# A 16-sequence cross-attention block on one core: the order of the first slots, of eight weight refills and of one pair of FFN gates

## The chip, the cores and the metric

One core of a Trainium2 chip runs the whole block. The metric is the device time of one launch in microseconds (us), the median of the runs. The kernel drives five engines by hand-written streams: TensorE (PE), VectorE (DVE), ScalarE (ACT), GpSimd (POOL) and SyncE (SP, which only issues transfers).

## The reference

For each of B = 16 sequences of S = 256 rows and D = 256 columns, with context `cond` of 256 rows and 192 columns (16 heads of 64, so 8 pairs of heads; everything is float32):

```
h = layernorm(x) * g1 + b1
x = softmax((h wq)(h wk)^T / 8) (h wv) wo + bo + x        # self attention
h = layernorm(x) * g2 + b2
x = softmax((h cq)(cond ck)^T / 8) (cond cv) co + cbo + x # cross attention
h = layernorm(x) * g3 + b3
a, gate = split(h w1 + fb1)                                # 1024 + 1024
out = (a * gelu(gate)) w2 + fb2 + x
```

Each float32 product is made on TensorE from rounded (high) and residual (low) parts in the type fp32r: three matmuls high x high, high x low, low x high. So every operand is written twice: once rounded (usually by ScalarE), once as the difference (VectorE or GpSimd).

## The kernel before

**Slots.** Attention is a software pipeline of `ATT` = 256 slots, one for each pair of heads of each sequence: 128 for self attention, 128 for cross attention. Slot c of an engine's stream holds that engine's part for several units at once. A unit k is the query and key product of one pair. In slot c, TensorE makes the scores of unit c (`pe_scores`), the query and key product of unit c + 3 (`pe_project`; later c + 7), a part of the values (`pe_value_turn`), the output product of unit c - 4 (`pe_outputs`), the transposes of the probabilities of c - 1 (`pe_transposes`), and probabilities times values of c - 2 (`pe_heads`). VectorE takes the maxima of the scores (`NM`), ScalarE the exponentials (`PT`, L791), TensorE transposes them into `PTB`, ScalarE rounds them into `PH` (L819), VectorE makes the low part `PL` (`dve_p_low`, L897). ScalarE and VectorE also copy and split each product into `QKS` (`act_copy_qk`, L722; `dve_split_qk`, L903). GpSimd normalizes the outputs (`ON` times `RB`, L1189) and splits them into `OT` (L1192, L1194), which `pe_outputs` reads.

**Two ways to the scores.** From unit 3 on (`DIRECT`), SP copies the parts of `QKS` with four transfers per unit into the ring `RX` (`copy_ring`, L683 and L685) in a layout with both parts stacked, and the scores read the ring. The units 0 to 2 are read straight from `QKS` (L454). `unit(k)` names the place in `QKS`; here units 2 and 3 have places of their own (0 and 1), so their products can be copied and split before the scores of units 0 and 1 are done.

**The first slots** run from c = -3. The weights arrive in twelve pieces, which are rounded by ScalarE (`act_weights`, L1526) and split by VectorE (`dve_weights`) and GpSimd (`pool_low`, L1559). The rows of sequence 1 go through the first layernorm beside them: statistics, `dve_normalize` (L858) into `XN`, a store to DRAM (`store_rows`, SP), a load that turns them (`act_load_rows`, four transfers on ScalarE's queue, L691), a transpose of 32 x 32 blocks (`dve_turn_rows`, L876), gain and bias (ScalarE), and the split into `HT` (`pool_split_h`, GpSimd). Unit 8 is the first to need them. Here the normalization lies behind the weight split of slot 0 for its first tile and in slot 1 for its second; the store is issued in slot 1, the load in slot 2, and the block transpose is in slot 3.

**The end of attention.** Weights for the next phase were split and stored to DRAM earlier. `fill_weights` (SP) refills `WQ` a quarter at a time, four chunks of 256 KB, one per slot (L1697). The quarters 2 and 3 for the FFN are refilled from slot `LAST` = 248 to 256, behind the ring copies in SP's order. The FFN processes chunks of two sequences in eight units each; `pe_gates(c)` makes both halves of unit c (4.2 us with its second product in the steady state), ScalarE's Gelu and VectorE turn them into `FH`, high and low (L1472, L1474), and `pe_second(s)` multiplies by `w2` (L1352). Units 0 to 3 are made early by `pe_raw` (L1295) in the last attention slots. Behind the last slot TensorE's order is written out by hand:

```
pe_gates(e, EARLY)
pe_heads(e, Slot(ATT + 1, ATT))
pe_outputs(e, ATT - 3)
pe_second(e, 0)
pe_second(e, 1)
pe_outputs(e, ATT - 2)
pe_gates(e, EARLY + 1)
```

What sets the order everywhere is the order in which each stream is written, with semaphores between the streams. SP, ACT and the others each run their stream in order, so an instruction that waits holds all behind it on its engine.

Of the kernel before, what the change touches and what calls it, by code (L numbers as in the profile page):

```python
# [19 lines left out]
PAIRS = H // 2  # L20
# [54 lines left out]
def first_alone(k):  # L75

    return 0 <= k < OLD
# [7 lines left out]
def joint(j):  # L85

    return OLD <= j < LAST
# [20 lines left out]
def unit(k):  # L108

    if last_alone(k):  # L110
        return (7, 1, 2, 0, 3, 4, 5, 6)[k - LAST]
    if alone(k):
        return k - 2 if DIRECT - 1 <= k <= DIRECT else (3, 7)[k % 2]
    n, p = place(k)
    u = n // 2 * PAIRS + p
    return 3 + u % 5 if n % 2 else u % 3
# [97 lines left out]
def block_kernel(nc, x, ctxt, ln1_g, ln1_b, ln2_g, ln2_b, ln3_g, ln3_b, sa_wq, sa_wk, sa_wv, sa_wo,  # L214
                 sa_bo, ca_wq, ca_wk, ca_wv, ca_wo, ca_bo, ff_w1, ff_b1, ff_w2, ff_b2, out):
    ctx = ExitStack()
    with ctx:
# [373 lines left out]

        def pe_slot(e, sl):
            c = sl.c
            late = c == 1 or joint(c + LEAD) and first_alone(c + AHEAD)
            if joint(c + LEAD):
                pe_project_both(e, c + LEAD)
            if c == 2:
                pe_value_turn(e, c)
            if first_alone(c + AHEAD) and not late:
                pe_project(e, c + AHEAD)  # L600
            if last_alone(c + LEAD):
                pe_project(e, c + LEAD)
            if ATT <= c + LEAD < ATT + RAWS:
                pe_raw(e, c + LEAD - ATT)

            if 0 <= c < ATT and not 2 <= c <= 3:
                pe_value_turn(e, c)
            if c == -2:
                pe_values(e, 0)

            pe_outputs(e, c - 4)
            pe_transposes(e, sl)

            if late:
                pe_project(e, c + AHEAD)

            pe_heads(e, sl)
# [94 lines left out]
        def act_copy_qk(e, k):  # L712

            e.wait_ge(a.pe_qk, nth_alone(k) + 1)
            if k >= LAST:
                held = max(m for m in range(DIRECT, k) if unit(m) == unit(k))
                e.wait_ge(d_dup[held % 2], 16 * COPIES * copied(held))
            elif k > DIRECT + 2:
                e.wait_ge(d_dup[k % 2], 16 * COPIES * copied(k - 2))
            elif k > DIRECT:  # L720
                e.wait_ge(a.pe_s, 2 * (k - DIRECT))
            e.activation(QKS[:, unit(k), 0:2, :], qk_bank(k)[:, :].rearrange("p (u s) -> p u s", u=2), ACT.Copy) \  # L722
                .then_inc(a.act_hi, 1)

# [30 lines left out]
        def act_slot(e, sl):  # L755
# [15 lines left out]
            if due(c, 1, 2):  # L771
                act_load_rows(e, due(c, 1), 0, 1)
            for k in range(KD):
                if due(c, 3 + k, 2):
                    act_gain_bias(e, due(c, 3 + k), k)
                if c == DIRECT + 1:
                    act_gain_bias(e, 1, k)
            for k in range(3):
                if due(c, k - 5, B):
                    act_load_ctx(e, due(c, k - 5, B), *((0,), (3,), (6, 7))[k])  # L780

            if sl.has(c):
                sl.wait(e, a.pe_t, c - 1)
# [12 lines left out]

            if c == 0:
                act_copy_qk(e, 2)
            if first_alone(c + AHEAD) and not late and c != -1:
                act_copy_qk(e, c + AHEAD)  # L800
            if joint(c + LEAD) and not late:
                act_copy_both(e, c + LEAD)
# [22 lines left out]
            if late:  # L825
                act_copy_qk(e, c + AHEAD)

            if due(c, 1, 2):
                act_load_rows(e, due(c, 1), 2, 3)
            if c == DIRECT - 1:  # L830
                act_load_rows(e, 1, 0, 1, 2, 3)
            for k in range(2):
                if due(c, k - 5, B):
                    act_load_ctx(e, due(c, k - 5, B), *((1, 2), (4, 5))[k])
# [94 lines left out]
        def dve_rows(e, sl):  # L929

            c = sl.c
            if due(c, 2, 2):
                dve_turn_rows(e, due(c, 2))
            if c == DIRECT:
                dve_turn_rows(e, 1)
            if due(c, -2, B):
                dve_turn_ctx(e, due(c, -2, B))
            n = normalized_in(c)
            if n:
                e.wait_ge(a.dve_th, n - 1)  # L940
# [32 lines left out]
            if ATT - 7 <= c < ATT - 3:  # L973
                dve_normalize(e, zero_ffn, fs, 1, ROWS, (c - ATT + 7,))

        def dve_reciprocal(e, sl, s):

            e.wait_ge(a.act_exp, 2 * s + 2)
            if s > 1:
                e.wait_ge(d_ds[(s - 2) % 4], 16 * ((s - 2) // 4 + 1))  # L980
            if s == 1:
                e.wait_ge(a.dve_rt, 1)
            e.reciprocal(RDEN[:, 0:4], DEN[:, s % 2, :]).then_inc(a.dve_rc, 1)
            e.wait_ge(a.dve_rc, s + 1)
            e.transpose(RDT[:, s % 2, :], RDEN[:, :]).then_inc(a.dve_rt, 1)

        def dve_slot(e, sl):
            c = sl.c
            late = joint(c + LEAD) and first_alone(c + AHEAD)
# [6 lines left out]
                                    AX.X, ALU.max, negate=True).then_inc(a.dve_nm, 1)  # L996

            if c == 0:
                dve_weights(e, 5)
                e.wait_ge(a.pe_h, 2)  # L1000
                dve_normalize(e, sl, a, 1, (near(1),), (0,))
                dve_split_qk(e, 2)
            if c == 1:
                dve_reciprocal(e, sl, 0)

            if c > 2 and sl.has(c - 2) and c < ATT - 1:
                dve_p_low(e, c - 2, 1)
# [9 lines left out]
            if 0 <= c + 1 < FIRST_V:  # L1017
# [1 line left out]
                sl.wait(e, a.pe_v, v + 1)  # L1019
                sl.wait(e, a.pl_v, v - 3)  # L1020
                e.tensor_copy(VF[:, v // 2 % 2, v % 2, :], VB[:, 0:S]).then_inc(a.dve_vf, 1)
            if c == 1:
                dve_normalize(e, sl, a, 1, (near(1),), (1,))
            if c == 2:
                dve_weights(e, 9)

            if late:
                dve_split_both(e, c + LEAD)
# [3 lines left out]
            dve_rows(e, sl)  # L1032
            dve_ffn_rows(e, c)

            if sl.has(c) and c > 0:
                dve_reciprocal(e, sl, c)

            if first_alone(c + AHEAD) and not late and c != -1:
                dve_split_qk(e, c + AHEAD)
            if joint(c + LEAD) and not late:  # L1040
                dve_split_both(e, c + LEAD)
# [114 lines left out]
        def pool_slot(e, sl):  # L1156
# [14 lines left out]
                if due(c, k - 1, B):  # L1171
                    pool_split_ctx(e, sl, due(c, k - 1, B), k)
            for k in range(KD):
                if due(c, 3 + k, 2):
                    pool_split_h(e, sl, due(c, 3 + k), k)
                if c == DIRECT + 1:
                    pool_split_h(e, sl, 1, k)
            pool_weights(e, c)
            for t in range(TT):
                if due(c, 5 + t):  # L1180
# [318 lines left out]
        def pe_attention_slot(e, sl):  # L1499
            if sl.c == -1:  # L1500
                pe_scores(e, Slot(0, ATT))
            if sl.c == 3:
                pe_value_turn(e, 3)
            if sl.c > 0:
                pe_scores(e, sl)
            pe_slot(e, sl)
# [22 lines left out]
        def dve_weights(e, *ns):  # L1529

            for n in ns:
# [5 lines left out]
                else:  # L1537
                    e.tensor_tensor(low, raw(n), hi, ALU.subtract).then_inc(s_wlo, 1)

        def act_attention_slot(e, sl):  # L1540
            act_slot(e, sl)
            if -AHEAD <= sl.c < 3:
                act_weights(e, *((4,), (5,), (6, 7), (8,), (9, 10), (11,))[sl.c + AHEAD])
            if sl.c == PAIRS * 2:
                e.wait_ge(d_sm, 16 * 5)
                e.activation(LNG[:, 1, :, :], LNG[:, 1, :, :], ACT.Copy, scale=SCALE).then_inc(s_gain, 1)
# [39 lines left out]
        def _(e):  # L1586
# [117 lines left out]
            def fill_weights(c):  # L1704
# [4 lines left out]
                if pair in HALVES and B + 1 <= seq <= B + 2 * NCH:  # L1709
                    store_split(QTR * NCH + 2 * (seq - B - 1) + HALVES.index(pair))  # L1710
                for phase, first in ((0, SLOTS), (1, ATT)):
                    for quarter in range(QTR):
                        if phase and quarter >= 2:
                            freed = nth_alone(ATT - QUAD + 2 * quarter - 3) + 1
                            at = LAST + 4 * (quarter - 2)
                            turns = ((0, 1, 2, 3), (0, 1, 3, 4))[quarter - 2]
                        else:
                            j = first - 2 * PAIRS + 4 * quarter + 3
                            freed = nth_joint(j) + 1
                            at = j - LEAD + 2  # L1720
                            turns = (0, 1, 2, 3)
                        for chunk in range(4):
                            if c == at + turns[chunk]:
                                if chunk == 0:
                                    await_stored(phase)
                                    e.wait_ge(a.pe_qk, freed)
                                    if quarter > 1:
                                        e.wait_ge(d_wq[quarter % 2], 16 * 4 * (QTR // 2 * phase + quarter // 2))
# [54 lines left out]
            for c in range(-AHEAD, ATT + 2):  # L1783
# [10 lines left out]
                if 0 <= c - 1 + AHEAD < ATT and c - 1 >= -AHEAD:  # L1794
                    k = c - 1 + AHEAD
                    if k >= DIRECT:
                        copy_ring(e, k)
                if c == 1:
                    store_rows(1)
                weights(c)  # L1800
                fill_weights(c)
# [81 lines left out]
        def _(e):  # L1883
# [12 lines left out]
            pe_heads(e, Slot(ATT + 1, ATT))  # L1896
            pe_outputs(e, ATT - 3)
            pe_second(e, 0)
            pe_second(e, 1)
            pe_outputs(e, ATT - 2)  # L1900
            pe_gates(e, EARLY + 1)
            pe_second(e, 2)
            pe_outputs(e, ATT - 1)
            pe_second(e, 3)
# [35 lines left out]
```

## Time and profile before

| | |
|---|---|
| median of 3 runs | 1690.47 us (1689.78 to 1691.63) |
| profiled execution, own time | 1689.77 us |
| its span | 1687.9 us |
| PE / DVE / ACT / POOL busy | 1676.3 / 1396.7 / 1249.1 / 1082.0 us |
| transfers | 288.91 MB, mean 171 GB/s |
| granted TensorE clock | 1.000 |

The span is from the first to the last instruction. A busy PE means that a matmul was in flight; the ends of matmuls are modelled, so that two that follow each other overlap by some 0.1 us, and the distance of starts is the better measure of what a group takes. "Idle before" is the time in which an engine had nothing in flight before an instruction, and the releaser is what ended it. Issues of transfers stand under ACTq and SPq with the time that they held the queue.

### The profile page before, as it was taken

What the parts mean: (1) busy time and instruction counts of PE and PEld (TensorE: products, weight loads), DVE (VectorE), ACT (ScalarE), POOL (GpSimd) and SP (SyncE); (2) the same over time, 40 slices, a digit from 0 to 9 for tenths busy, and PEclk for the clock granted to TensorE, in tenths of its full rate; (3) what the DMA queues carried; (4) which work ended last, traced back from release to release, by engine and by line L of the source; (5) the groups of instructions that cost most, each with busy time, mean ns of one, the idle gap of its engine ahead of it and who ended that gap; (6) DMA issues with size and microseconds to landing.
All of it is one profiled execution on the core that took longest, in us unless ns stands there. A gap on an engine that the chain in (4) does not pass through costs nothing.

```text
span 1687.9 us, 39061 instructions
## 1 busy us (share of the span) xinstructions
PE 1676.3 (99%) x11712; PEld 1560.7 (92%) x11712; DVE 1396.7 (83%) x2964; ACT 1249.1 (74%) x3378; POOL 1082.0 (64%) x1804
## 2 busy tenths in 40 slices
PE   8999999999999999999999999999999999999999
PEld 8999999999999999999999999999999998888888
DVE  7888788888888888888888888888888987656665
ACT  7788788888888888888888888888888886232221
POOL 7776577777766667687777777777777564231111
PEclk9999999999999999999999999999999999999999
DMA  7776677777776667887787878787776776112110
GB/s 209 187 181 161 171 197 198 205 202 212 198 181 158 158 166 201 233 221 181 192 211 188 210 198 209 195 207 187 191 188 173 196 209 169 51 50 76 62 39 26
DMA packets 301137, 288.91 MB, mean 171 GB/s; under 512 B 103424, under 2 KB 252032, under 8 KB 300928
## 3 DMA queue, kind: packets, MB, share of 16 engines
q1 hardware_dynamic: 246848, 272.76, 61.9%
q10 hardware_dynamic: 54080, 13.65, 3.6%
q8 instruction: 96, 1.57, 0.4%
q14 instruction: 113, 0.93, 0.2%
HBM read 82.98 MB, written 37.49 MB: 71 GB/s over the span
## 4 chain that ended last, share of the span: by engine, by line
PE 96%; DVE 1%; DMA 1%; SPq 0%; issue 0%; ACT 0%; ACTq 0%; DVEq 0%
PE QKB L564 17%; PE PVB L648 14%; PE PTB L577 13%; PE WOP L630 11%; PE VB L499 9%; PE S L466 7%; PE S L467 7%; PE S L1330 5%; PE PTB L1330 5%; PE QKB L546 3%; PE QKB L1352 3%; PE VB L1352 3%; PE QKB L1295 0%; DMA XR<-in_x_dram 0%; DMA HF<-rows 0%
## 5 line engine op out<-in xcount | busy, mean ns | idle before, releaser
L791 ACT ACTIVATE PT<-S,NM 128x256 f32<-128x256 f32 x1024 | 471.9, 473 | 139.2 <-DVE NM L995 138.5
L897 DVE TENSOR_TENSOR PL<-PTB,PH 128x512 fp32r<-128x512 f32 x512 | 350.8, 686 | 123.8 <-ACT PH L819 122.3
L1189 POOL TENSOR_TENSOR ON<-ON,RB 128x256 f32<-128x256 f32 x256 | 188.5, 736 | 272.2 <-DVE ON L1014 247.8
L995 DVE TENSOR_REDUCE NM<-S 128x2 f32<-128x512 f32 x512 | 327.4, 681 | 1.2 <-PE S L467 1.1
L819 ACT ACTIVATE PH<-PTB 128x1024 fp32r<-128x1024 f32 x256 | 264.0, 1031 | 72.0 <-PE PTB L577 71.1
L577 PE MATMUL PTB<-IDN,PT 128*128 128x128 f32 x2048 | 265.5, 272 | 0.6 <-DVE PL L897 0.5
L466 PE MATMUL S<-RX 128*128 128x256 f32 x1012 | 254.0, 283 | 2.1 <-DMA RX<-QKS 2.1
L467 PE MATMUL S<-RX 128*128 128x256 f32 x1012 | 253.7, 283 | 0.0
L564 PE MATMUL QKB<-HT,WQ 128*128 128x512 f32 x936 | 242.0, 394 | 0.2
L630 PEld LDWEIGHTS WOP<-WO,OT 128*128 128x128 f32 x1536 | 217.5, 190 | 19.7
L577 PEld LDWEIGHTS PTB<-IDN,PT 128*128 128x128 f32 x2048 | 229.6, 140 | 1.3 <-DVE PL L897 0.8
L630 PE MATMUL WOP<-WO,OT 128*128 128x256 f32 x1536 | 224.0, 282 | 0.0
L1014 DVE TENSOR_TENSOR ON<-PVB,ON 64x256 f32<-64x256 f32 x512 | 213.5, 417 | 3.9 <-ACT ON L766 0.3
L766 ACT ACTIVATE ON<-PVB 64x256 f32<-64x256 f32 x512 | 194.5, 380 | 17.9 <-issue 3.1
L791 ACT ACTIVATION_READ_ACCUMULATOR PT<-S,NM 128x1 f32 x1024 | 207.5, 203 | 0.0
L1194 POOL TENSOR_TENSOR OT<-ON,OT 128x256 fp32r<-128x256 f32 x256 | 190.3, 744 | 20.5
L1168 POOL TENSOR_TENSOR VR<-VF,VR 128x256 fp32r<-128x256 f32 x256 | 189.8, 741 | 20.5
L466 PEld LDWEIGHTS S<-RX 128*128 128x128 f32 x1012 | 193.4, 191 | 2.5 <-DMA RX<-QKS 2.5
L467 PEld LDWEIGHTS S<-RX 128*128 128x128 f32 x1012 | 194.2, 192 | 0.0
L564 PEld LDWEIGHTS QKB<-HT,WQ 128*128 128x128 f32 x936 | 165.9, 189 | 27.8 <-DVE QKS L911 0.6
L648 PE MATMUL PVB<-PH,VR 128*128 128x256 f32 x1024 | 183.5, 300 | 0.4 <-issue 0.4
L648 PE MATMUL PVB<-PL,VR 128*128 128x256 f32 x1024 | 163.4, 282 | 0.0
(162 smaller groups left out, 2921.8 us busy)
## 6 DMA issues: line engine op xcount, KB each, us to landing
RX<-QKS SPq DMA_DIRECT2D x506, 192.0 KB, 2.9
RX<-QKS SPq DMA_DIRECT2D x506, 128.0 KB, 2.8
RB<-denominators SPq DMA_DIRECT2D x512, 64.0 KB, 2.7
out_dram<-XR SPq DMA_DIRECT2D x32, 256.0 KB, 3.4
weights_qk<-SPL SPq DMA_DIRECT2D x32, 256.0 KB, 3.4
WQ<-weights_qk SPq DMA_DIRECT2D x32, 256.0 KB, 3.3
rows<-XN SPq DMA_DIRECT2D x23, 256.0 KB, 2.7
rows<-HF SPq DMA_DIRECT2D x22, 256.0 KB, 2.7
```

Source lines behind the costliest of these rows:

```text
L466: e.matmul(o, q, RX[:, c % 2, i, K1, :], start=True, stop=False)
L467: last = e.matmul(o, q, RX[:, c % 2, i, K2, :], start=False, stop=True)
L564: last = e.matmul(QKB[:, :], w_pair(w, wp, p), act, start=i == 0, stop=i == len(passes) - 1)
L577: last = e.transpose(PTB[:, i, kt * S + qt * P:kt * S + (qt + 1) * P], PT[:, s % 2, q0:q0 + P], IDN[:, :])
L630: last = e.matmul(WOP[:, t * D:(t + 1) * D], OT[:, op, t * P:(t + 1) * P], WO[:, p, wp, :], start=begins(s) and t == 0 and j == 0, stop=en ...
L648: last = e.matmul(PVB[:, i * S:(i + 1) * S], VR[:, s // 2 % 2, kt, s % 2, i * P:(i + 1) * P], part[:, first:first + S], start=i == 0 and j ...
L766: last = e.activation(ON[OWN[i], s % 2, :], PVB[OTHER[i], i * S:(i + 1) * S], ACT.Copy)
L791: last = e.activation(PT[:, c % 2, j * S:(j + 1) * S], S1[:, i, qt * S:(qt + 1) * S], ACT.Exp, bias=NM[:, j:j + 1], accum_out=DEN[:, c % 2 ...
L819: e.activation(PH[:, s % 2, :], PTB[:, :, :].rearrange("p i n -> p (i n)"), ACT.Copy) \
L897: e.tensor_tensor(PL[:, cols], PTB[:, i, :], PH[:, s % 2, cols].bitcast(F32), ALU.subtract).then_inc(a.dve_pl, 1)
L995: e.tensor_reduce(NM[:, i * TT:(i + 1) * TT], S1[:, i, :].rearrange("p (t s) -> p t s", t=TT), AX.X, ALU.max, negate=True).then_inc(a.dve_ ...
L1014: last = e.tensor_tensor(on, PVB[OWN[i], i * S:(i + 1) * S], on, ALU.add)
```

## The change

- `unit`: all of the first units alternate between the places 3 and 7 of `QKS`; a copy of unit k > 1 now waits for the scores of unit k - 2.
- TensorE: in slot 2 the product of unit 5 goes behind the transposes, as that of unit 4 does in slot 1; the values of slot 2 and 3 stand in their general place.
- ScalarE: the copies of units 3 and 4 stand ahead of the exponentials of slots 1 and 2. The load of the rows of sequence 1 is at the end of slot 1; gain and bias in slots 3 and 4.
- VectorE: in slot 0 both tiles of sequence 1 are normalized right behind the maxima; the low parts of units 3 and 4 stand behind the maxima of slots 1 and 2; the reciprocal of slot 0 is in slot 0; the block transpose is in slot 2.
- SP: the store of the rows of sequence 1 is the first instruction of its slots. GpSimd: `pool_split_h` in slots 3 and 4.
- The last eight `WQ` transfers are issued by ScalarE at the end of its slots 248 to 255 (`act_load_last`).
- `pe_second(e, 1)` stands behind `pe_outputs(e, ATT - 2)` and `pe_gates(e, EARLY + 1)`.

```diff
@@ unit
-        return k - 2 if DIRECT - 1 <= k <= DIRECT else (3, 7)[k % 2]
+        return (3, 7)[k % 2]
@@ pe_slot
-            late = c == 1 or joint(c + LEAD) and first_alone(c + AHEAD)
+            late = 0 < c < DIRECT or joint(c + LEAD) and first_alone(c + AHEAD)
-            if c == 2:
-                pe_value_turn(e, c)
...
-            if 0 <= c < ATT and not 2 <= c <= 3:
+            if 0 <= c < ATT:
                 pe_value_turn(e, c)
@@ act_copy_qk
-            elif k > DIRECT + 2:
+            elif k > DIRECT + 1:
                 e.wait_ge(d_dup[k % 2], 16 * COPIES * copied(k - 2))
-            elif k > DIRECT:
-                e.wait_ge(a.pe_s, 2 * (k - DIRECT))
+            elif k > 1:
+                e.wait_ge(a.pe_s, 2 * (k - 1))
@@ act_slot
+            if 0 < c < DIRECT:
+                act_copy_qk(e, c + 2)
...
-            if first_alone(c + AHEAD) and not late and c != -1:
+            elif first_alone(c + AHEAD) and not late and not -1 <= c < DIRECT - 1:
                 act_copy_qk(e, c + AHEAD)
...
-            if due(c, 1, 2):
-                act_load_rows(e, due(c, 1), 2, 3)
-            if c == DIRECT - 1:
-                act_load_rows(e, 1, 0, 1, 2, 3)
+            if due(c, 1):
+                act_load_rows(e, due(c, 1), *(range(2, 4) if due(c, 1, 2) else range(4)))
@@ dve_rows
-            if due(c, 2, 2):
+            if due(c, 2):
                 dve_turn_rows(e, due(c, 2))
-            if c == DIRECT:
-                dve_turn_rows(e, 1)
@@ dve_slot
             if c == 0:
+                e.wait_ge(a.pe_h, 2)
+                dve_normalize(e, sl, a, 1, (near(1),))
                 dve_weights(e, 5)
-                e.wait_ge(a.pe_h, 2)
-                dve_normalize(e, sl, a, 1, (near(1),), (0,))
-                dve_split_qk(e, 2)
-            if c == 1:
-                dve_reciprocal(e, sl, 0)
+            if 0 < c < DIRECT:
+                dve_split_qk(e, c + 2)
+            if c == 2:
+                dve_weights(e, 9)
...
-            if c == 1:
-                dve_normalize(e, sl, a, 1, (near(1),), (1,))
-            if c == 2:
-                dve_weights(e, 9)
...
+            if c == 0:
+                dve_split_qk(e, 2)
+            elif first_alone(c + AHEAD) and not late and not -1 <= c < DIRECT - 1:
                 dve_split_qk(e, c + AHEAD)
@@ pool_slot
-                if due(c, 3 + k, 2):
+                if due(c, 3 + k):
                     pool_split_h(e, sl, due(c, 3 + k), k)
-                if c == DIRECT + 1:
-                    pool_split_h(e, sl, 1, k)
@@ scalar stream
+        def act_load_last(e, c):
+
+            quarter, chunk = divmod(c - LAST, 4)
+            if 0 <= quarter < 2:
+                if chunk == 0:
+                    for done in d_ws:
+                        e.wait_ge(done, 16 * QTR * NCH)
+                    e.wait_ge(a.pe_qk, nth_alone(ATT - QUAD + 2 * quarter + 1) + 1)
+                    e.wait_ge(d_wq[quarter], 16 * 4 * (QTR // 2 + 1))
+                e.dma_start(WQ[:, 2 + quarter, chunk, :, :].bitcast(F32), WSQ[1, :, 2 + quarter, chunk, :, :]) \
+                    .then_inc(d_wq[quarter], 16)
+
         def act_attention_slot(e, sl):
             act_slot(e, sl)
+            act_load_last(e, sl.c)
@@ sync stream
-                if c == 1:
+                if c == -AHEAD:
                     store_rows(1)
@@ fill_weights
-                    for quarter in range(QTR):
-                        if phase and quarter >= 2:
...
+                    for quarter in range(QTR - 2 * phase):
@@ tensor stream
             pe_second(e, 0)
-            pe_second(e, 1)
             pe_outputs(e, ATT - 2)
             pe_gates(e, EARLY + 1)
+            pe_second(e, 1)
             pe_second(e, 2)
```

## Rows read from the trace of the kernel before

**Rows 1.** The page: busy time of each engine.

```profile
PE 1676.3 (99%) x11712; PEld 1560.7 (92%) x11712; DVE 1396.7 (83%) x2964; ACT 1249.1 (74%) x3378; POOL 1082.0 (64%) x1804
```

**Rows 2.** TensorE's waits over the span: releaser, us in total, times, longest.

```profile
PE S L466 <- DMA RX<-QKS: 2.1, 2, 1.1
PE QKB L1352 <- DVE QKS L1474: 2.0, 1, 2.0
```

**Rows 3.** TensorE's timeline, first slots: start, us, line, out<-in, [idle before].

```profile
19.78 1.68 PE L546 MATMUL QKB<-HT,WQ 128*128 128x256 f32 x12
...
23.21 1.60 PE L546 MATMUL QKB<-HT,WQ 128*128 128x256 f32 x12
...
27.19 0.29 PE L466 MATMUL S<-RX 128*128 128x256 f32 x1
...
34.00 0.39 PE L466 MATMUL S<-RX 128*128 128x256 f32 x1 [0.97 <-DMA RX<-QKS]
...
35.81 1.69 PE L546 MATMUL QKB<-HT,WQ 128*128 128x256 f32 x12 [0.60 <-DVE QKS L903]
...
40.61 0.28 PE L466 MATMUL S<-RX 128*128 128x256 f32 x1
```

**Rows 4.** VectorE's timeline, first slots.

```profile
15.81 1.37 DVE L858 TENSOR_SCALAR XN<-XR,MV,RSTD 128x256 f32<-128x256 f32 x1
...
18.04 0.68 DVE L903 TENSOR_TENSOR QKS<-QKB,QKS 128x512 fp32r<-128x512 f32 x1
18.64 1.27 DVE L995 TENSOR_REDUCE NM<-S 128x2 f32<-128x512 f32 x2
19.84 0.16 DVE L983 RECIPROCAL RDEN<-DEN 128x4 f32<-128x4 f32 x1
...
20.47 0.40 DVE L858 TENSOR_SCALAR XN<-XR,MV,RSTD 128x256 f32<-128x256 f32 x1
...
34.16 0.71 DVE L876 STREAM_TRANSPOSE XN<-HF 128x512 f32<-128x512 f32 x1 [1.96 <-DMA HF<-rows]
```

**Rows 5.** ScalarE's timeline with its queue (ACTq), end of slot 2.

```profile
26.96 0.34 ACTq L691 DMA_DIRECT2D HF<-rows  x1
...
27.34 2.04 ACTq L691 DMA_DIRECT2D HF<-rows  x3
29.43 0.63 ACT L1526 ACTIVATE WV<-XR 128x512 fp32r<-128x512 f32 x1 [1.05 <-issue]
```

**Rows 6.** Stretches: busy us of each engine, granted clock, DMA share, GB/s.

```profile
16.00:20.00 4.00, 3.28 (x33) 2.90 (x32) 4.00 (x7) 2.53 (x8) 3.84 (x6) 1.00 0.10 32
...
28.00:32.00 4.00, 3.22 (x24) 2.59 (x23) 3.73 (x8) 2.89 (x9) 3.08 (x6) 1.00 0.98 247
```

**Rows 7.** SP's queue, first slots: the last copy of unit 4.

```profile
28.65 0.62 SPq L685 DMA_DIRECT2D RX<-QKS  x1
```

**Rows 8.** GpSimd's timeline, first slots.

```profile
30.14 1.27 POOL L1559 TENSOR_TENSOR WV<-XR,WV 128x512 fp32r<-128x512 f32 x1 [0.76 <-ACT WV L1526]
...
33.88 0.73 POOL L1189 TENSOR_TENSOR ON<-ON,RB 128x256 f32<-128x256 f32 x1
```

**Rows 9.** TensorE's timeline, end of attention.

```profile
1407.56 0.39 PE L466 MATMUL S<-RX 128*128 128x256 f32 x1 [1.10 <-DMA RX<-QKS]
...
1430.25 0.98 PE L1352 MATMUL QKB<-WV,QKS 128*128 128x256 f32 x6 [2.01 <-DVE QKS L1474]
```

**Rows 10.** SP's queue, end of attention: the last copy of unit 254, a refill.

```profile
1403.85 0.62 SPq L685 DMA_DIRECT2D RX<-QKS  x1
1404.64 0.46 SPq L1697 DMA_DIRECT2D WQ<-weights_qk  x1
```

**Rows 11.** ScalarE's timeline with its queue, end of attention.

```profile
1390.75 0.35 ACTq L1364 DMA_DIRECT2D rows<-XN  x1
1390.79 0.77 ACT L766 ACTIVATE ON<-PVB 64x256 f32<-64x256 f32 x2
```

**Rows 12.** GpSimd and VectorE behind the last slot.

```profile
1427.31 0.74 POOL L1194 TENSOR_TENSOR OT<-ON,OT 128x256 fp32r<-128x256 f32 x1
...
1429.51 0.69 DVE L1474 TENSOR_TENSOR QKS<-PT,QKS 128x512 fp32r<-128x512 f32 x1
```

More of the change, by code:

```diff
@@ L773, in act_slot @@
             for k in range(KD):
-                if due(c, 3 + k, 2):
+                if due(c, 3 + k):
                     act_gain_bias(e, due(c, 3 + k), k)
-                if c == DIRECT + 1:
-                    act_gain_bias(e, 1, k)
             for k in range(3):
@@ L974, in dve_ffn_rows @@
                 dve_normalize(e, zero_ffn, fs, 1, ROWS, (c - ATT + 7,))
[L976 to L985, printed above, removed]
         def dve_slot(e, sl):
@@ L1033, in dve_slot @@
             dve_ffn_rows(e, c)
-            if sl.has(c) and c > 0:
-                dve_reciprocal(e, sl, c)
-            if first_alone(c + AHEAD) and not late and c != -1:
+            if sl.has(c):
+                sl.wait(e, a.act_exp, 2 * c + 2)
+                if c > 1:
+                    e.wait_ge(d_ds[(c - 2) % 4], 16 * ((c - 2) // 4 + 1))
+                e.reciprocal(RDEN[:, 0:4], DEN[:, c % 2, :]).then_inc(a.dve_rc, 1)
+                sl.wait(e, a.dve_rc, c + 1)
+                e.transpose(RDT[:, c % 2, :], RDEN[:, :]).then_inc(a.dve_rt, 1)
+            if c == 0:
+                dve_split_qk(e, 2)
+            elif first_alone(c + AHEAD) and not late and not -1 <= c < DIRECT - 1:
                 dve_split_qk(e, c + AHEAD)
@@ L1173, in pool_slot @@
             for k in range(KD):
-                if due(c, 3 + k, 2):
+                if due(c, 3 + k):
                     pool_split_h(e, sl, due(c, 3 + k), k)
-                if c == DIRECT + 1:
-                    pool_split_h(e, sl, 1, k)
             pool_weights(e, c)
@@ L1501, in pe_attention_slot @@
                 pe_scores(e, Slot(0, ATT))
-            if sl.c == 3:
-                pe_value_turn(e, 3)
             if sl.c > 0:
@@ L1711, in fill_weights @@
                 for phase, first in ((0, SLOTS), (1, ATT)):
-                    for quarter in range(QTR):
-                        if phase and quarter >= 2:
[L1714 to L1721, printed above, removed]
+                    for quarter in range(QTR - 2 * phase):
+                        j = first - 2 * PAIRS + 4 * quarter + 3
+                        freed = nth_joint(j) + 1
                         for chunk in range(4):
-                            if c == at + turns[chunk]:
+                            if c == j - LEAD + 2 + chunk:
                                 if chunk == 0:
@@ L1727, in fill_weights @@
                                     if quarter > 1:
-                                        e.wait_ge(d_wq[quarter % 2], 16 * 4 * (QTR // 2 * phase + quarter // 2))
+                                        e.wait_ge(d_wq[quarter % 2], 16 * 4)
                                 load_quarter(phase, quarter, chunk)
```

## Prediction

> **What bounds the kernel now.** I read the page first, then TensorE's list of waits, then the timelines of every engine in the first 45 us and from 1370 to 1440 us, and TensorE's row for the middle. The page has PE busy 99% of the span [rows 1], and the granted clock is 1.00 in every stretch asked for [rows 6]: nothing can be gained but PE's own stalls, and only edits that make or remove a stall count. The waits name them: two on the copied units `RX`, one of 2.0 us before a second FFN product [rows 2], and smaller ones of up to 0.6 us. The timelines put all of these either before 41 us or between 1407 and 1431 us. Steady slots are gapless; the slot that starts at 40.61 us is the first of them [rows 3]. So the change, which touches the slots -3 to 4 and the end of attention, is judged at two marks: when the scores of slot 5 start (40.61 us before), and when `pe_gates(EARLY + 1)` and what follows it run. All arithmetic is against the profiled execution: its span is 1687.9 us and its own time 1689.77; the median of the runs shown is 1690.47, 0.7 above it.
>
> **The first slots.** Nothing is touched until slot 0's maxima. Every figure below is a start or an end in us, chained from the rows.
>
> *VectorE, slot 0.* Now both normalizations of sequence 1 come right behind the maxima, from about 15.0. One took 1.37 us there while GpSimd ran, the other 0.40 us [rows 4]. How long the two take in a row is not shown: 0.8 us at best, 2.75 at worst. I take 1.37 + 0.40, because the first lies in the same stretch of GpSimd's weight splits as before. Against before, this slot gets the second tile (0.40) and the reciprocal with its transpose (19.84 to 20.17, 0.33), and loses the split of unit 3 (18.04 to 18.64, 0.60) [rows 4]: the maxima of slot 1 start at 18.64 + 0.40 + 0.33 - 0.60 = 18.77 instead of 18.64, and I leave the exponentials behind them where they were (19.4 to 21.3). The Trainium skill's page "SBUF — State Buffer", section "Who interferes with whom", says that a vector operation in a two-port mode and a GpSimd operation block each other for the whole instruction. The 1.37 us row agrees; by the rule alone the second tile could be held as well, which is the upper bound above.
>
> *Low part of unit 3 behind the maxima.* It is no longer made ahead of slot 1's maxima but behind them: these take 1.20 (18.64 to 19.84 [rows 4]), so it runs from 19.95 to 20.6. The product of unit 4 waits for it: 20.6 instead of 19.78 [rows 3], a loss of 0.8. The scores of slot 2 follow one product (1.44) later, at 22.05.
>
> *ScalarE at the end of slot 1.* The four transfers that fetch the rows of sequence 1 now issue here, behind the rounding of the probabilities. Before, they held ScalarE's queue from 26.96 to 29.38, 2.4 us, and ScalarE resumed at 29.43 [rows 5]. Now they go from 21.0 (the exponentials' last instruction) to 23.4. They wait for the store of these rows, which SP can issue at 16.8 in a stretch in which the transfer engines are 10% busy [rows 6]; so no wait there. SP is held in its first slot until then, and has nothing else queued. Behind the issues ScalarE does two weight roundings (one takes 0.63 [rows 5], two overlapped 1.15) until 24.55, then, new, the copy of unit 4 ahead of the exponentials of slot 2: 24.6 to 25.2. Its low part ends at 25.9, and the product of unit 5, which PE now has behind the transposes, starts there instead of at 23.21. PE has the values and the transposes in between (until 24.7), so it stalls 1.2. Product 1.44 and heads 1.03 give the scores of slot 3 at 28.4 (27.19 before): 1.2 late, the sum of what the edits cost until here.
>
> *What comes back.* (a) Before, VectorE sat 1.96 us, until 34.16, for the fetched rows [rows 4]; they landed 4.7 us behind their last issue, with the transfer engines 98% busy [rows 6]. Now the last issue ends at 23.4, so at the same 4.7 us they are there at 28.1, and VectorE passes at about the time when the copy of unit 5 lets it split anyway (28.1 to 28.75). (b) The last `RX` copy of unit 4 was issued at 28.65 and landed at 34.0 [rows 3, 7]. Now SP issues the four from 25.9 to 28.4, as it has one store less in front. With the same 4.7 us they land at 33.1. (c) PE: scores until 29.35, product of unit 6 until 30.8, values 31.5, transposes 32.3 (low part of slot 1's probabilities done 31.55, so the 0.5 us stall goes), heads 33.35, scores of slot 4 at 33.35 instead of 34.00. (d) The product of unit 7 waited 0.6 until 35.81, because unit 6 was split behind the late rows [rows 3, 4]. Now the exponentials of slot 3 end at 32.95, copy and split follow until 34.45, and the product starts at 34.5. It ends at 35.95, the values at 36.65. (e) GpSimd gets the rounded weights 0.45 later, loses the 0.76 us that it waited before 30.14, and has one half of `pool_split_h` (1.15) in slot 3 instead of 4: the first normalized output, 33.88 before [rows 8], comes 0.84 later, at 34.7, and its low part, two operations on, at 36.75. So `WOP` starts at 36.8, and the scores of slot 5 at 39.35 against 40.61. The first slots gain **1.2 us**. Bounds: with normalizations of 0.40 each 1.0 more (-2.2); with 1.37 each 1.0 less, or with rows that land 0.9 later, which holds VectorE as long; together a loss of 0.7. So -2.2 to +0.7. What lies between 40.61 and 1370 us has no gap and no edit.
>
> **The last eight refills.** SP issued one `WQ` transfer in each of eight slots from 248, about 0.6 us of its queue. It ran behind: the last `RX` copy of unit 254 went out from 1403.85 to 1404.47, and PE waited 1.10 us for it until 1407.56 [rows 9, 10]. Four refills lie ahead of these copies, so the queue reaches them some 2.1 us earlier (a little less than 4 x 0.6) and they land, at 3 us, at 1405.4, before PE is there (1406.46). Gain **1.1 us**; bounds 0 and 1.15. On ScalarE the issues are new. Each follows a 1.03 us rounding whose execution covers 0.6 us of issue: with the two `rows` stores there, the copy behind started 0.04 us after the issue began [rows 11]. Besides, ScalarE waits 0.64 us per slot for maxima. So they cost nothing; without cover eight would cost 4.8. Their waits (a product of two slots ago, transfers long landed) are all met. The first use of the refilled quarters is at 1422, four slots later.
>
> **Gates of unit 5 ahead of the second product of unit 1.** PE stalled 2.01 us, until 1430.25, for the low part of `FH` [rows 9]. Now `pe_outputs(ATT - 2)` (0.72) and the gates (2.78) fill in between: second product of unit 0 until 1428.15, outputs until 1428.9, gates until 1431.7, by when the low part (done 1430.20) is 1.5 us old [rows 12]. The outputs need GpSimd's low part, done 1428.05 [rows 12], 0.1 ahead. The low parts of the next units were done 0.4 us and more ahead of where PE would now ask for them, by the same timelines. The stall goes whole: **2.0 us**, bounds 1.7 and 2.01. Behind it PE runs gapless to its end, so the gain stays.
>
> **Sum.** 1689.77 - 1.2 - 1.1 - 2.0 = 1685.5 for an execution like the profiled one; against the median, 1690.47 - 4.3 = **1686.2 us**. A difference under 0.2%, 3.4 us, can't be told from none here. The ends of the terms give -5.4 and -1.0.
>
> **The rivals.**
> 1. *The copies land late all the same* (within 0.2%). The eight refills still move 256 KB each, now beside the `RX` copies instead of behind them: the one at 1400.7 would overlap the copies of unit 254. 256 KB at the 247 GB/s of a full stretch [rows 6] are 1.1 us: 1405.4 becomes 1406.5, just at PE's arrival, and a landing slower by 1 us more takes the whole term. If the first slots give nothing either, 1690.47 - 2.0 = 1688.5; with their 1.2, 1687.3. For it: the transfer engines have been 98% busy with such traffic [rows 6]. Against: the 2.1 us of lead. The Trainium skill's page "DMA: Bandwidth & Descriptors", section "Issuing engines are not separate DMA queues", says that transfers from either engine share the same 16 engines and that only issue time is saved; no row here shows two full queues side by side. Chance 0.25.
> 2. *ScalarE is held by the refills* (slower). A refill that holds ScalarE beyond 1.0 (rounding) + 0.64 (its wait) delays the exponentials and PE. At 2.6 us each, eight cost 8 x 1.0 = 8 us, less 3.2 for the other terms: 1695.3. It makes the kernel slower than before from 1.64 + 3.2 / 8 = 2.04 us each on. Only the 0.68 us per issue of three in a row [rows 5] speaks for it, the two single ones [rows 11] against. Chance 0.08.
> 3. *The first slots go better*: short normalizations, copies that land in 3 us. 1690.47 - 5.4 = 1685.1. Chance 0.15.
> 4. My forecast 0.52.
>
> The range for 8 in 10 is 1684.3 to 1689.6. Faster by over 0.2% (up to 1687.1): 0.62, all of 3 and 0.47 of 4; within 0.2%: 0.29; slower: 0.09, rival 2 and 0.01 for what I don't see.
>
> **What would show it.** Right: PE's scores of slot 5 at 39.4; waits of about 0.9 and 1.2 us before the products of units 4 and 5; none on `RX`; no PE wait before any second FFN product; refill issues on ScalarE's queue of 0.6 us with the exponentials' starts unmoved; gates of unit 5 at 1428.9 less the earlier gains. Wrong: a VectorE wait of over 1 us for the rows in slot 2, an `RX` wait near 1404 us, a wait of `WOP` on GpSimd at the end, or any wait in the middle.

## The result, and the profile after

The changed kernel takes 1685.63 us (median of 10 runs, 1685.17 to 1687.62) against 1690.65 us (10 runs, 1687.74 to 1692.01): ratio 0.9977, 95% interval 0.9969 to 0.9985, so 2.5 to 5.2 us less. Forecast was 1686.2. Two things stand in the run lists before any trace is opened. The gain is 5.0 us where my three terms gave 4.3; but in three later series (79 runs) the kernel before had medians of 1689.05, 1689.66 and 1689.52, so 1690.65 stands high, and against those the gain is 3.4 to 4.0. And the changed kernel is steadier: 2.5 us from fastest to slowest, where before had 4.3. The profiled execution of the changed kernel took 1686.2 us itself, with a span of 1684.4 (1687.9 before).

TensorE's timeline after, first slots (start, us, line, out<-in, [idle before]), answers to [rows 3]: the products of units 4 and 5, the scores of slots 3, 4 and 5.

```profile
20.22 1.67 PE L546 MATMUL QKB<-HT,WQ 128*128 128x256 f32 x12 [0.83 <-DVE QKS L900]
...
25.00 1.69 PE L546 MATMUL QKB<-HT,WQ 128*128 128x256 f32 x12 [0.41 <-DVE QKS L900]
...
27.48 0.28 PE L466 MATMUL S<-RX 128*128 128x256 f32 x1
...
32.65 0.28 PE L466 MATMUL S<-RX 128*128 128x256 f32 x1
...
38.51 0.28 PE L466 MATMUL S<-RX 128*128 128x256 f32 x1
```

The two new waits are there, 0.83 and 0.41 us. Of the old ones behind slot 3 none is left: slot 5 starts at 38.51 instead of 40.61. VectorE's timeline answers to [rows 4]: both normalizations took 1.81 us (1.77 reckoned), and the block transpose of the fetched rows starts at 26.18 with no idle time noted before it, instead of 34.16 behind 1.96.

```profile
14.43 1.81 DVE L855 TENSOR_SCALAR XN<-XR,MV,RSTD 128x256 f32<-128x256 f32 x2
...
26.18 0.70 DVE L873 STREAM_TRANSPOSE XN<-HF 128x512 f32<-128x512 f32 x1
```

ScalarE's timeline with its queue, end of slot 1, answers to [rows 5]. The first three of the four fetches are issued while the exponentials run, the fourth beside the rounding of the probabilities (20.79), and the weight roundings start at 21.69, right behind that rounding: nothing was held.

```profile
19.58 0.34 ACTq L689 DMA_DIRECT2D HF<-rows  x1
...
20.92 0.45 ACTq L689 DMA_DIRECT2D HF<-rows  x1
21.69 1.17 ACT L1510 ACTIVATE WQ<-XR 128x512 fp32r<-128x512 f32 x2
```

At the end of attention the scores of unit 254 come without a wait (against 1.10 in [rows 9]). In ScalarE's timeline of that stretch a refill is issued beside the rounding, the copy follows as ever, and the exponentials have their 0.64 us of idle time as before, where the row of the slot ahead reads

```profile
1403.13 0.48 ACT L791 ACTIVATE PT<-S,NM 128x256 f32<-128x256 f32 x1 [0.64 <-DVE NM L995]
```

TensorE's row after, then ScalarE's:

```profile
1405.15 0.28 PE L466 MATMUL S<-RX 128*128 128x256 f32 x1
```

```profile
1404.40 1.02 ACT L818 ACTIVATE PH<-PTB 128x1024 fp32r<-128x1024 f32 x1
1404.41 0.36 ACTq L1533 DMA_DIRECT2D WQ<-weights_qk  x1
1405.45 0.77 ACT L764 ACTIVATE ON<-PVB 64x256 f32<-64x256 f32 x2
1406.87 0.47 ACT L790 ACTIVATE PT<-S,NM 128x256 f32<-128x256 f32 x1 [0.64 <-DVE NM L979]
```

SP's queue shows the last copy of unit 254 going out 7.15 us ahead of its scores (1405.15), where before it was 3.7 (1403.85 in [rows 10], 1407.56 in [rows 9]):

```profile
1398.00 0.62 SPq L683 DMA_DIRECT2D RX<-QKS  x1
```

Behind the last slot, TensorE's timeline (the gates of unit 5, then the second products of units 2 and 3) and, of the same stretch, VectorE's and GpSimd's:

```profile
1426.42 2.91 PE L1316 MATMUL PTB<-HT,WQ 128*128 128x512 f32 x12
...
1431.02 0.98 PE L1338 MATMUL QKB<-WV,QKS 128*128 128x256 f32 x6 [0.26 <-DVE QKS L1460]
...
1433.77 0.98 PE L1338 MATMUL QKB<-WV,QKS 128*128 128x256 f32 x6 [0.34 <-DVE QKS L1460]
```

```profile
1428.97 0.85 DVE L1458 CAST QKS<-PT 128x512 fp32r<-128x512 f32 x1
1429.85 1.11 DVE L1460 TENSOR_TENSOR QKS<-PT,QKS 128x512 fp32r<-128x512 f32 x1
1430.89 1.22 DVE L1454 SCALAR_TENSOR_TENSOR PT<-VF,B,PT 128x512 f32<-128x512 f32 x1
```

```profile
1428.35 4.36 POOL L1059 TENSOR_TENSOR XR<-XR,BOUT 128x256 f32<-128x256 f32 x4
```

The 2.01 us stall of [rows 9] is gone and two small ones have come. I had none there. GpSimd's four bias sums, which before began at 1434.53, now run in the middle of VectorE's steps, and both take longer than they did before:

```profile
1430.90 0.43 DVE L1472 CAST QKS<-PT 128x512 fp32r<-128x512 f32 x1
1431.36 0.69 DVE L1474 TENSOR_TENSOR QKS<-PT,QKS 128x512 fp32r<-128x512 f32 x1
1434.53 2.82 POOL L1071 TENSOR_TENSOR XR<-XR,BOUT 128x256 f32<-128x256 f32 x4
```

The middle of attention, where no line was changed, is not equal in the two executions: slot 154 starts 2.38 us earlier than before, slot 213 only 1.12, and no wait of TensorE stands between them. One other kernel below, the one without the refills on ScalarE's queue, loses 1.15 us between the same slots; in the rest the shift is 0.3 us or less. One profile of each kernel is therefore not enough to read a term of 1 us from; several traces of the same piece of code, and the medians, are.

### The profile page after: what moved, and what is told of

The parts are those of the page before. It is cut to its first block, busy times and chain, and to the rows that moved or that the text cites. A ratio compares the mean times of both kernels' runs of the same rounds, so it can differ in the third digit from the quotient of the medians.

```text
span 1684.4 us, 39061 instructions
## 1 busy us (share of the span) xinstructions
PE 1675.8 (99%) x11712; PEld 1559.7 (93%) x11712; DVE 1398.6 (83%) x2964; ACT 1248.2 (74%) x3378; POOL 1082.8 (64%) x1804
## 3 DMA queue, kind: packets, MB, share of 16 engines
q8 instruction: 96, 1.57, 0.4%
## 4 chain that ended last, share of the span: by engine, by line
PE 96%; DVE 2%; ACT 1%; issue 0%; ACTq 0%; DMA 0%; POOL 0%; DVEq 0%; POOLq 0%
PE QKB L564 17%; PE PVB L646 14%; PE PTB L577 13%; PE WOP L628 11%; PE VB L499 9%; PE S L467 7%; PE S L466 7%; PE S L1316 5%; PE PTB L1316 5%; PE QKB L546 3%; PE QKB L1338 3%; PE VB L1338 3%; PE QKB L1281 1%; ACT PT L790 0%; DVE NM L979 0%
```

## The experiments

Eleven more runs were made, the last of them the kernel before once more. The first three make one part of the change each, on the kernel before.

**First slots alone** (only the last eight refills and the gates as before).

> The first slots of the change alone; refills and gates as before. My theory (the three edits are local and add up): the scores of slot 5 start at about 38.5 us (40.6 before) and the median falls by 2.1 to 2.3 us against the kernel before; the waits on RX near 1407 us (1.1) and before the second product of unit 1 (2.0) stay. Rival (the gain of the first slots is handed back later, since the middle of the changed kernel gave back 1.2 us of the lead): slot 5 early by 2.1 us but the median less than 1.2 us lower.

Measured: 1688.85 us (11 runs), before 1689.05 (28 runs); ratio 0.9996 (0.9987 to 1.0005). Slot 5 started at 38.55, as expected, and the `RX` wait (0.79) and the 2.00 us stall stayed, but the median shows hardly a gain. The trace says why this execution had none: its windows behind the stall (busy us of PE, PEld, DVE, ACT, POOL, then granted clock, DMA share, GB/s).

```profile
1426.00:1428.00 2.00, 0.69 (x6) 0.48 (x4) 1.90 (x4) 0.72 (x1) 1.62 (x2) 1.00 0.00 0
1428.00:1430.00 2.00, 1.32 (x11) 1.32 (x12) 1.93 (x4) 0.62 (x1) 0.00 (x0) 1.00 0.48 132
1430.00:1432.00 2.00, 2.00 (x11) 1.98 (x10) 1.93 (x4) 0.07 (x1) 0.02 (x1) 0.50 0.47 130
1432.00:1434.00 2.00, 2.00 (x7) 1.55 (x6) 1.08 (x2) 0.00 (x0) 1.92 (x3) 0.65 0.03 8
```

Behind the stall TensorE's clock was 0.50, then 0.65 over the next window: 1.2 GHz instead of 2.4 for about 3.4 us. The gates took 3.58 us from start to start there and 2.75 in the first profile. By that the lead over the kernel before, 1.57 us at the end of the stall, was 0.01 us at TensorE's end. Part of the lead had gone earlier: it was 2.05 us at slot 127 and 1.47 at slot 128, where the product waited 0.34 us for VectorE, as also happened, with 0.16 and 0.20 us, in two later traces with the new first slots.

The mean granted clock that is noted for every run says how often this happened: it was below 1.000 in 10 of these 11 runs, and in 15 of the 28 of the kernel before. Among the runs below 1.000 the medians are 1689.09 and 1690.14 us. That suggests that the first slots gain about 1.0 us here and that the plain medians hide it, because more of these runs had the slow clock; why more had it is not shown.

**Refills alone.**

```diff
-                    for quarter in range(QTR):
+                    for quarter in range(QTR - 2 * phase):
...
+            act_load_last(e, sl.c)
```

> The last eight refills on ScalarE's queue alone. My theory (SP's queue was late because of them): no wait on RX at unit 254, the issues hold ScalarE for nothing, 1.1 us less. Rival (the 16 transfer engines are shared, so the copies land as late as before): wait of 0.5 us or more stays, less than 0.6 us gained. Rival (ScalarE held): the exponentials' idle time before them changes from 0.64 us and the median is higher.

Measured: 1689.11 us (11 runs); ratio 1.0001 (0.9992 to 1.0010). The wait on `RX` had moved from unit 254 to 253, and the slow clock was there too:

```profile
1396.62 0.62 SPq L685 DMA_DIRECT2D RX<-QKS  x1
```

```profile
1402.33 0.39 PE L466 MATMUL S<-RX 128*128 128x256 f32 x1 [1.23 <-DMA RX<-QKS]
```

```profile
1430.00:1432.00 2.00, 2.00 (x14) 2.00 (x15) 1.93 (x4) 0.69 (x1) 0.00 (x0) 0.73 0.48 137
1432.00:1434.00 2.00, 2.00 (x9) 1.80 (x9) 1.90 (x4) 0.00 (x0) 0.54 (x2) 0.50 0.25 72
```

From 1388 to 1403 us the `RX` copies landed after 3.2 / 4.3 / 5.7 us (min, median, max); in the changed kernel, 1388 to 1400, after 2.5 / 3.1 / 4.4. The last copy of unit 253 left SP's queue at 1397.24 and landed only at 1402.33, so SP's order was not its cause. By the mark set for it the rival "shared transfer engines" holds in this execution; which transfers held the copy up is not shown.

**Gates alone.**

```diff
             pe_second(e, 0)
-            pe_second(e, 1)
             pe_outputs(e, ATT - 2)
             pe_gates(e, EARLY + 1)
+            pe_second(e, 1)
```

> Only the second product of unit 1 behind the gates of unit 5. My prediction: the stall of 2.0 us goes whole, 2.0 us less. Rival, from the trace of the changed kernel (GpSimd's bias sums start 6 us earlier, run beside VectorE's FFN steps and slow them, so that two new waits of 0.26 and 0.34 us appear): 1.4 us less, with waits of 0.2 to 0.4 us before the second products of units 2 and 3.

Measured: 1688.20 us (11 runs), ratio 0.9992 (0.9983 to 1.0001). The waits before the second products of units 2 and 3 were 0.26 and 0.33 us: the rival read from the trace is right, the stall shrinks by 1.4 us, not 2.0. The medians show 0.85 us of it, with 1.5 us to either side. All 11 runs had a clock of 1.000, and against the 13 such runs of the kernel before (median 1687.88) no gain is left; why the shorter stall doesn't show there stays open.

**The changed kernel with the bias sums held back.**

```diff
+            e.wait_ge(fs.dve_hl, EARLY)
             pool_add_bias(e, zero_ffn, fs, 0)
```

> The changed kernel, with GpSimd's first FFN bias sums held back until the low part of unit 3 is made. If these sums are what slows VectorE there: its steps for units 2 and 3 take 0.75, 0.43 and 0.69 us instead of 1.22, 0.85 and 1.11, no wait before second products, 0.6 us less than the changed kernel, 5.0 to 5.6 less than the kernel before. If the rounding of the output of unit 255 (OT) is what slows it: steps for unit 2 stay long, at most 0.3 us less.

Measured: 1684.71 us (6 runs, 1684.34 to 1686.98), ratio 0.9975 (0.9964 to 0.9987), so 4.3 us less than the kernel before of this series where 5.0 to 5.6 were expected; against the changed kernel 0.9 less where 0.6 was expected. No wait before any second product. The second and third of VectorE's steps for unit 2 are short again, as are the steps for unit 3; the first still ran beside GpSimd's split of the last output and stayed at 1.22.

```profile
1427.38 1.22 DVE L1454 SCALAR_TENSOR_TENSOR PT<-XN,B,PT 128x512 f32<-128x512 f32 x1
1428.64 0.43 DVE L1458 CAST QKS<-PT 128x512 fp32r<-128x512 f32 x1
1429.10 0.69 DVE L1460 TENSOR_TENSOR QKS<-PT,QKS 128x512 fp32r<-128x512 f32 x1
1429.71 0.75 DVE L1454 SCALAR_TENSOR_TENSOR PT<-VF,B,PT 128x512 f32<-128x512 f32 x1
```

So the sums are the cause of the two waits. This kernel has no 2 us stall and its times are tight; the other parts were taken back from it, not added to the noisy kernel before.

**Without the first slots** (refills, gates and late sums on the kernel before).

> Refills, gates and late bias sums, but the first slots of before. There is no stall of 2 us behind attention here, so no slow TensorE clock. My theory (the first slots are worth 1.3 us: slot 5 starts at 39.8 to 40.0 in undisturbed traces of the old slots and at 38.5 in the new): 1686.0 us, that is 1.3 over the kernel with all edits (1684.7). Rival (worth 2.1 to 2.3, as the two first profiles differ): 1686.9. Rival (handed back in the middle): 1685.0 or less.

Measured: 1686.11 us (11 runs; before 1689.66), ratio 0.9983 (0.9974 to 0.9992); slot 5 at 39.57. Against 1684.71 above, and 1684.56 of a kernel of the same series below, the first slots are worth 1.4 to 1.55 us.

**Without the refills on ScalarE's queue.**

> First slots, gates and late bias sums, but the last eight refills on SP's queue as before. My theory: the wait on RX at unit 254 comes back with 0.7 to 1.1 us and the time is 1685.6. Rival (the transfer engines are the limit, not SP's issue time; with the refills alone on ScalarE a wait of 1.2 us stood at unit 253): the wait is there or not by chance and the time within 0.3 us of 1684.7.

Measured: 1685.89 us (11 runs), ratio 0.9976 (0.9967 to 0.9985), 1.2 to 1.3 us over the same two. In the profiled execution, the slowest of these 11 (1686.66), the wait is back where it was:

```profile
1406.63 0.39 PE L466 MATMUL S<-RX 128*128 128x256 f32 x1 [0.77 <-DMA RX<-QKS]
```

**Refills on SP, behind the last `RX` copies.**

```diff
-                            turns = ((0, 1, 2, 3), (0, 1, 3, 4))[quarter - 2]
+                            turns = ((5, 5, 6, 6), (3, 4, 4, 5))[quarter - 2]
```

> All edits and late bias sums, but the last eight refills stay on SP, issued behind the last RX copies (slots 253 to 257). They leave the stretch in which the copies of units 250 to 255 are in flight, and ScalarE issues nothing. If SP's order in front of the copies was the cost: no RX wait, 1684.7, the same as with ScalarE's queue. If ScalarE's issues cost something: less than 1684.4. If the late refills hold the gates of unit 6: a new wait on WQ near 1435 us.

Measured: 1684.56 us (8 runs, 1683.94 to 1686.74), ratio 0.9972 (0.9962 to 0.9982). No `RX` wait at the end, no wait on `WQ`. It equals the refills on ScalarE within 0.15 us, so ScalarE's issues cost nothing that can be measured. This is the fastest kernel of the study, 1.1 us below the changed one by the medians, which is less than the medians of one kernel differ between series (1689.05 to 1690.65 for the kernel before).

**Of the first slots only the earlier rows** (places of units 2 and 3, copies, low parts and products as before).

```diff
-                dve_weights(e, 5)
                 e.wait_ge(a.pe_h, 2)
-                dve_normalize(e, sl, a, 1, (near(1),), (0,))
+                dve_normalize(e, sl, a, 1, (near(1),))
+                dve_weights(e, 5)
...
-                if c == 1:
+                if c == -AHEAD:
                     store_rows(1)
```

> All edits and late bias sums, but of the first slots only the earlier rows of sequence 1; the places of units 2 and 3, the order of copies, low parts and products as before. If the gain of the first slots is the rows alone: slot 5 at 38.5 us or earlier, no waits before the products of units 4 and 5 (0.8 and 0.4 with all edits), time 1684.7 or down to 1683.7. If the low parts behind the maxima are what helps: slot 5 at 39 us or later, time 1685.3 or more.

Measured: 1686.86 us (11 runs), ratio 0.9985 (0.9976 to 0.9994): no better than the kernel without any of it (1686.11). Slot 5 at 40.18. The wait for the rows is gone, but TensorE waits elsewhere: 0.59 us for a value copy, 0.40 for the split of unit 5, 0.19 and 0.43 around the heads, and in slot 4 for the exponentials, which the earlier work on VectorE had pushed back:

```profile
34.04 0.36 PE L466 MATMUL S<-RX 128*128 128x256 f32 x1 [0.41 <-ACT PT L789]
```

**Of the first slots only the order** (rows of sequence 1 as late as before).

> All edits and late bias sums, but the rows of sequence 1 as late as before; places, order of copies, low parts and products of the first slots as changed. If both parts of the first slots are needed (rows alone gave nothing: 1686.9, slot 5 at 40.2): VectorE waits for the rows near 34 us again, slot 5 at 39.5 us or later, 1685.8 or more. If the order alone is the gain: slot 5 at 38.5, 1684.7.

Measured: 1686.34 us (11 runs; before 1689.52), ratio 0.9985 (0.9976 to 0.9994), slot 5 at 39.59. VectorE waits for the rows again and the product of unit 7 for VectorE:

```profile
33.15 0.71 DVE L877 STREAM_TRANSPOSE XN<-HF 128x512 f32<-128x512 f32 x1 [1.40 <-DMA HF<-rows]
```

```profile
34.79 1.69 PE L546 MATMUL QKB<-HT,WQ 128*128 128x256 f32 x12 [1.11 <-DVE QKS L904]
```

Neither half alone gains; both together gain 1.4. This execution also had an `RX` wait of 0.40 us at unit 254 with the refills on ScalarE's queue; its last copy went out only at 1402.17, 3.7 us ahead of the scores.

**The changed kernel with the stall put back** (only the gates' order).

> The changed kernel with only the order of the gates taken back: the 2.0 us stall is there again. By my first reckoning (the stall alone) it is 2.0 us less the 0.6 us of the two new waits: 1.4 us over the changed kernel, 1687.0. By the theory from the last traces (after such a stall TensorE's granted clock falls to 0.5 for some 3 us in part of the executions, 1.6 us more): runs spread over 3 us or more, median 1687.5 to 1688.7, and if the profiled run shows it, products at half pace just behind the stall.

Measured: 1687.57 us (11 runs, 1686.23 to 1690.16), ratio 0.9989 (0.9980 to 0.9998). That is 1.9 us over the changed kernel, and its runs spread over 3.9 us instead of 2.5. The spread alone proves little, since the kernel with only the order, which has no stall, spreads as far (1685.33 to 1689.20). The stall (2.00) stands in the trace; the clock was 1.00 in this, its fastest execution. The clock noted for every run tells more: it was below 1.000 in 4 of the 11 (median 1688.91 us, the other seven 1687.42). Over all timed runs it was below 1.000 in 66 of 112 of the kernels that have the 2.0 us stall (the kernel before in its three later series, first slots alone, refills alone, and this one), and in none of the 79 of the kernels without it. So in these runs the slow clock came only with the stall, and not always.

**The kernel before once more.**

> The kernel before once more, for a second profile. If the slow clock behind the 2.0 us stall is a matter of chance: either 1.00 throughout, or 0.5 for some 3 us behind 1430 us and a time 1.6 us longer. The RX wait of slot 4 (0.97 us in its first profile, 0 to 0.43 in other kernels with the same slots) differs again.

Measured: 1689.16 us, one run. Clock 1.00. `RX` waits of 0.87 in slot 4, 0.35 at unit 253 and 0.48 at unit 255, none at 254; slot 5 at 40.03.

## Why the prediction was right, step by step

*That only TensorE's stalls count* held: busy PE is 1675.8 us after and 1676.3 before, and the marks I named moved: slot 5 from 40.61 to 38.51 (39.4 forecast), the gates of unit 5 to 1426.42 (1428.9 less the 2.3 us of the earlier terms, 1426.6).

*First slots, 1.2 us forecast; 1.3 to 1.55 measured.* The first profile overstated it (2.10), since its slot 5 at 40.61 was the latest of five traces of the old slots (39.57, 39.82, 39.99, 40.03, 40.61). The six with the new slots lie from 38.51 to 38.85: 1.3 us between the medians, as the timed pairs say. Of the steps, the wait of 0.8 before the product of unit 4 is right to 0.03. The wait before that of unit 5 was put at 1.2 and is 0.41: I let ScalarE's queue begin its four issues only at the exponentials' last instruction, and let them hold ScalarE. They went out under the exponentials and the rounding behind them, from 19.58 on, so the copy of unit 4 began at 22.93 instead of 24.6, and VectorE's maxima, not ScalarE, set the start. From slot 3 on everything is 0.7 to 0.9 us earlier than reckoned (slot 4 32.65 against 33.35, slot 5 38.51 against 39.35). That the forecast of the gain still holds is luck: the baseline of 40.61 was late by about as much (0.6), so two errors of one size cancelled. That both halves are needed I had not asked; the two half kernels show it.

*Refills, 1.1 us forecast; 1.2 to 1.3 measured.* Every one of the five traces with the eight refills in front of the copies on SP has `RX` waits at the end (1.10, 0.79, 0.74, 0.77, and 0.35 with 0.48). Of seven with the refills on ScalarE's queue five have none, one 0.40 and one 1.23. Behind the copies there was none in one trace. SP's queue tells more than the waits. With the refills in front, the last copy of unit 254 went out 3.2 to 4.0 us ahead of its scores in all five traces; in the five without a wait it was 5.1 to 7.2, and 7.15 with the refills behind the copies. So my cause, SP's order, is borne out. Its size was wrong: I gave SP's queue 2.1 us, and it came 5.85 us earlier, of which 1.15 are the lead that this slot had anyway. The sum did not feel it, since no more than the wait could be won. The two waits that came all the same have two causes. In the trace with 0.40 SP's queue was late again (3.7 us ahead) though it held no refill; what held it is not shown. In the one with 1.23 the copy went out 5.7 us ahead and landed late: that is the first rival, in one of seven. The Trainium skill's page "DMA: Bandwidth & Descriptors", section "Issuing engines are not separate DMA queues", gives only issue time to a second queue. The traces agree in so far as what changed is when SP's queue came to the copies. They don't show that the refills slowed the landing: with the refills behind the copies the median landing time from 1388 to 1403 us was 3.0 us, with them on ScalarE's queue it was 3.1 with the sums held back and 4.3 with the refills alone. Rival 2, ScalarE held, is refuted by the 0.64 us of idle time and by the kernel that leaves the refills to SP at the same time.

*Gates, 2.0 us forecast; 1.9 measured (by medians of two series, so uncertain by about 1 us), from two causes of which I named one; that the size agrees is luck.* The step that failed is "the low parts of the next units were done 0.4 us and more ahead ... by the same timelines". It took VectorE's timeline as fixed, though the same edit frees the last output 6 us earlier, and with it GpSimd's bias sums, which slow VectorE. The stall gives 1.4 us (2.01 less 0.26 and 0.34). The sums held back gave the rest, 0.6 in the trace and 0.9 by medians of different series. The other 0.5 us of the measured 1.9 I put down to the slow clock: seen in two of five profiled executions that have the stall (first slots alone, refills alone) and in none of the eight without it, at some 1.6 us each. Two fifths of 1.6 are 0.6. That the clock fell only with the stall is shown by the count over all timed runs (66 of 112 against none of 79). Its share of the 1.9 is not: by means, the runs with the stall put back and a clock of 1.000 lie 1.2 us over the changed kernel (1687.14 against 1685.97) and the four below 1.000 another 2.0 higher, which makes 1.2 + 4/11 of 2.0, or 1.9; but by medians the seven at 1.000 are already 1.8 over it.

*The sum.* The parts taken back one at a time give 1.4 + 1.25 + 1.9 = 4.6 us (the first two from the kernel with the sums held back); the direct comparison gives 5.0, or 3.4 to 4.0 if the later medians of the kernel before are used (1689.05, 1689.66, 1689.52). Added singly to the kernel before they gave 0.2, -0.1 and 0.9, each with 1.5 us to either side. That is below their values in the full kernel, and still within the intervals; for the refills only just (1.25 against an upper end of 1.35). The slow clock probably hid one of them: more runs of the first slots alone had it than of the kernel before. For the rest it stays open whether the parts help each other (fewer late copies when TensorE and SP keep another distance) or the noise hid them.

## What to carry to other kernels

- When an edit lets an engine start a side job earlier, look at what that job will run beside: here 4.4 us of GpSimd sums slid under VectorE's critical steps and took back 0.6 of 2.0 us, and one added wait, on VectorE's count of low parts, returned it.
- Measure small parts by taking them out of the best kernel, not by adding them to the first: with its stall and its chance waits gone, six of the eight runs of the fastest one lay within 0.5 us, and parts of 1.2 to 1.9 us could be told apart.
- Read the mean granted clock of every run beside its time: here it was below 1.000 in 66 timed runs, where the traces showed the fall twice.
- Where two waits lie in a row behind each other, one half of a reordering can be worth nothing: rows alone 1686.86 us and order alone 1686.34 against 1686.11 with neither, and 1684.6 with both.

## What the runs showed of the hardware

- A stall of 2.0 us of an otherwise full TensorE was followed, in two of five profiled executions, by about 3.4 us at a granted clock of 0.50 (1.2 GHz), which began 1.0 to 1.3 us behind the end of the stall. Over all timed runs the mean granted clock was below 1.000 in 66 of 112 with the stall and in none of 79 without. The other waits, 1.5 us at the start and up to 1.23 us later, were followed by a clock of 1.00 in all traces.
- ScalarE's queue issued four transfers while exponentials and a rounding of the same engine ran (19.58 to 21.37); none of them delayed an operation. The same four issues took 2.4 us in [rows 5], where ScalarE sat 1.05 us behind them.
- VectorE's cast of 128 x 512 took 0.43 us without GpSimd's sums and 0.85 beside them, its subtraction 0.69 and 1.11, its multiply with bias 0.75 and 1.22. The four sums took 2.82 us before and 4.36 beside these steps.
